# Attention on one core: five of a head's eight low probability halves on GpSimd instead of four

## The reference

```python
h = layer_norm(x, g1, b1)
q, k, v = (h @ wq1), (h @ wk1), (h @ wv1)            # 16 heads of 64
sim = einsum('bhid,bhjd->bhij', q, k) * D_HEAD ** -0.5   # 1024 x 1024 per head
attn = softmax(sim, axis=-1)
out = einsum('bhij,bhjd->bhid', attn, v)
x = x + out @ wo1 + bo1
```

## Time and profile before

| | |
|---|---|
| median of 3 runs | 2682.14 us (2680.29 to 2689.24) |
| the profiled execution | 2685.46 us, its span 2683.7 us |
| TensorE busy | 2270.3 us (85%) |
| VectorE busy | 1770.8 us (66%) |
| ScalarE busy | 1586.9 us (59%) |
| GpSimd busy | 1234.0 us (46%) |
| self-attention, four stretches | 353, 354, 357 and 352 us |
| in these 1416 us: TensorE, VectorE, ScalarE, GpSimd busy | 1308.8, 1143.4, 1113.8, 834.8 us |
| granted TensorE clock there | 0.98, 0.99, 0.98, 1.00 |

### The profile page before, as it was taken

How to read it: one execution, slowest core, us unless ns; L and a number is a source line. 1 busy time by engine, 2 the same in 40 slices (tenths; PEclk the granted TensorE clock), 3 DMA queues, 4 the chain that set the end, 5 groups by cost and what they waited for, 6 DMA issues and landing times.

```text
span 2683.7 us, 58442 instructions
## 1 busy us (share of the span) xinstructions
PE 2270.3 (85%) x24644; PEld 1437.8 (54%) x24644; DVE 1770.8 (66%) x3202; ACT 1586.9 (59%) x2124; POOL 1234.0 (46%) x756
## 2 busy tenths in 40 slices
PE   5999987779699998777869999877797999987778
PEld 2566655455365655445526665554553666554455
DVE  5888874644688887464358888746446888874643
ACT  2877774633477777363237777736334777772632
POOL 2555562640265556264026555626402655561640
PEclk8999998889799999797969999988897999997979
DMA  2212110210212121020022221102102121210200
GB/s 64 70 45 70 45 47 9 58 33 1 57 49 68 47 57 35 18 63 19 16 65 59 56 59 49 42 9 58 33 1 58 49 68 47 60 32 20 61 19 16
DMA packets 64021, 116.26 MB, mean 43 GB/s; under 512 B 16758, under 2 KB 21008, under 8 KB 63760
## 3 DMA queue, kind: packets, MB, share of 16 engines
q1 hardware_dynamic: 63760, 112.52, 16.1%
HBM read 50.77 MB, written 2.10 MB: 20 GB/s over the span
## 4 chain that ended last, share of the span: by engine, by line
PE 55%; DVE 16%; issue 7%; ACT 6%; DMA 6%; POOL 5%; SPq 4%; POOLq 2%; DVEq 0%; ACTq 0%
PE scores L687 7%; PE scores L688 6%; PE scores L689 6%; PE work L764 6%; PE scores L806 5%; PE scores L795 5%; DVE minima L1123 4%; SPq L519 3%; DVE prob L1146 3%; PE work L826 3%; PE work L830 3%; PE work L687 3%; PE work L689 3%; PE work L688 3%; PE work L828 3%
## 5 line engine op out<-in xcount | busy, mean ns | idle before, releaser
L654 POOL TENSOR_TENSOR prob<-prob 128x1024 f16<-128x1024 f32 (+1 forms) x320 | 689.3, 2155 | 753.4 <-ACT prob L990 741.1
L1123 DVE TENSOR_REDUCE minima<-work 128x1 f32<-128x512 f32 x1024 | 685.8, 685 | 112.4 <-PE work L764 97.7
L989 ACT ACTIVATE prob<-scores 128x1024 f32<-128x1024 f32 (+1 forms) x576 | 592.4, 1028 | 280.9 <-PE scores L806 258.3
L990 ACT ACTIVATE prob<-scores 128x1024 f16<-128x1024 f32 (+1 forms) x576 | 588.8, 1022 | 0.0
L826 PE MATMUL work<-vals,prob 128*128 128x65 f16 (+1 forms) x4608 | 497.1, 195 | 62.0 <-POOL prob L654 53.5
L826 PEld LDWEIGHTS work<-vals,prob 128*128 128x128 f16 (+1 forms) x4608 | 438.2, 100 | 134.6 <-POOL prob L654 67.1
L830 PE MATMUL work<-vals,prob 128*128 128x65 f16 (+1 forms) x4608 | 497.1, 197 | 0.0
L828 PE MATMUL work<-vals,prob 128*128 128x64 f16 (+1 forms) x4608 | 497.1, 195 | 0.0
L828 PEld LDWEIGHTS work<-vals,prob 128*128 128x128 f16 (+1 forms) x4608 | 436.0, 98 | 59.0 <-issue 2.9
L764 PE MATMUL work<-ka,qa 128*128 128x512 f16 x1024 | 406.2, 400 | 66.9 <-DMA kb<-staged_k 37.5
L830 PEld LDWEIGHTS work<-vals,prob 128*128 128x128 f16 (+1 forms) x4608 | 436.3, 99 | 0.0
(11 more groups left out here) (127 smaller groups left out, 4015.8 us busy)
## 6 DMA issues: line engine op xcount, KB each, us to landing
raw_odd<-in_pieces SPq DMA_DIRECT2D x40, 512.0 KB, 3.8
raw_even<-in_pairs SPq DMA_DIRECT2D x53, 384.0 KB, 3.2
qa<-staged_q SPq DMA_DIRECT2D x128, 128.0 KB, 2.3
ka<-staged_k SPq DMA_DIRECT2D x128, 128.0 KB, 2.3
qb<-staged_q SPq DMA_DIRECT2D x64, 128.0 KB, 2.3
kb<-staged_k SPq DMA_DIRECT2D x64, 128.0 KB, 2.4
qa<-qa SPq DMA_DIRECT2D x64, 128.0 KB, 2.3
raw_odd<-in_pairs SPq DMA_DIRECT2D x13, 384.0 KB, 3.2
```

Of the source, the lines that this page charges most:

```text
L654: pool.tensor_tensor(prob[1][0:kr, slot, :], prob32[0:kr, slot, :], prob[0][0:kr, slot, :], ALU.subtract).then_inc(a.polished, 1)
L989: act.activation(prob32[0:kr, n % shape.ring, :], source, ACT.Exp)
L990: act.activation(prob[0][0:kr, n % shape.ring, :], source, ACT.Exp)\
L1123: dve.tensor_reduce(minima[:, t, h:h + 1], out[:, :], AX.X, ALU.max, negate=True)\
```

## The change

The set of tiles whose low half GpSimd makes goes from (1, 3, 5, 7) to (0, 3, 4, 5, 7). VectorE makes those of tiles 1, 2 and 6 instead of 0, 2, 4 and 6. The list of steps is the same; only the engine of tiles 0, 1 and 4 changes.

```diff
 RING, LAG = 4, 3
-SELF = Shape("self", TILES, P, 2, 2, 1, (1, 3, 5, 7))
+SELF = Shape("self", TILES, P, 2, 2, 1, (0, 3, 4, 5, 7))
 CROSS = Shape("cross", 1, CTX, 1, 2, 2, ())
```

## The result

| | before | after |
|---|---|---|
| median of 15 runs each, taken side by side | 2681.20 us (2670.77 to 2694.55) | 2691.93 us (2687.75 to 2702.05) |
| the profiled execution | 2685.46 us | 2701.96 us |
| VectorE busy, GpSimd busy | 1770.8, 1234.0 us | 1713.3, 1404.2 us |
| TensorE's clock in the four self-attentions | 0.98, 0.99, 0.98, 1.00 | 0.99, 0.99, 0.98, 0.98 |

The changed kernel is slower by a ratio of 1.0045 (95% interval 1.0028 to 1.0061), that is 12 us (7.5 to 16.4). Forecast were 8.5 and a time of 2690.5. VectorE has lost 57 us of work and GpSimd has gained 170; the time follows neither sum, as expected.

What follows compares the result with a forecast made beforehand. TensorE is what the rest waits on, itself waiting for key DMA, max-reduces, shifts and GpSimd's low halves. Terms 24 - 18.5 + 8 - 3 - 2 = +8.5 us on the runs' median 2682.14 gave 2690.5 us, range 2666 to 2722.

Steps and rivals of the forecast that it cites:

- First heads: 24 first heads of pairs: tile 1's subtraction ahead of the gather delays TensorE's value product by 1.0 us each, +24 us.
- the earlier row: Row of shifts goes out 0.7 us earlier at each head's end; a few heads wait for it, -2 us.
- The two races: First heads: tile 1's subtraction finds GpSimd free, tile 2's starts before polish 3; both margins 0.1 to 0.2 us.
- Second heads: 28 heads: step 3's excess goes, -23 us; later delays at the head's end +4.5; term -18.5, between -28 and -4.
- nothing won later in VectorE comes back: First heads: step 7's first max waits for the key DMAs, so tile 4's subtraction leaving step 5 gains nothing.
- The first head of a round: 4 heads: split now behind polish 0 delays tile 1's and possibly tile 2's subtraction; +8 us, between 3 and 13.
- The last pair: 4 heads, first one bound by GpSimd: fewer subtractions get between, -1.0 at best; term -3 us, between -4 and +3.
- the race at polish 3: Rival: GpSimd goes before tile 2's subtraction in all 24 first heads, +41 us, about 2731 us; chance 0.11.
- The value product: Rival: in first heads its slack covers the gather's delay, the +24 goes, sum -15.5, 2666.5 us; chance 0.16.
- The 85 us of freed VectorE time: Rival: the 64 subtractions leaving VectorE count in full, 85 us, giving 2597 us; chance 0.03.
- The shared way as the bound: Rival: each head adds 0.91 us of exclusive VectorE/GpSimd use, +58 us, 2740 us; chance 0.04.
- The clock's rival: Rival: a second idle microsecond brings TensorE's half-speed clock in 20 more first heads, +32 on top, 2722 us; chance 0.10.

Runs made afterwards that it cites:

- the thin splits: Kernel before, with the three 1024-wide split instructions (L595 to L599) done on 32 columns only: 2621.59 us, ratio 0.9788.

## Why the prediction was right, step by step

The time and the sign were right, and so was the mechanism of the two big terms, the refine ahead of the gather in first heads and the split in front of tile 0 in second heads. Tile 4's effect in second heads had no term, and that the single terms come out as close as they do is in part luck.

- **First heads**, +24 and -2 for the earlier row: measured +22.3 with both. The gather came 1.13 later and the weight load 1.00, as worked out, in 24 of 24. The fifth exponential came only 0.81 later, 24 x 0.81 = 19.4, because the weight load is the wrong mark: before, it ran 0.21 ahead of the value product's first matmul, which waited its turn on TensorE; now it runs 0.03 ahead. From the gather's end to that matmul there were 0.46 us (2295.23 to 2295.69), of which 0.15 are the hand-over (2310.61 to 2310.76), so the slack was 0.31, and the matmul came 1.13 - 0.31 = 0.82 later in all 24. In the kernel before, and then in the changed one:

```profile
2295.69 0.19 PE L826 MATMUL work<-vals,prob 128*128 128x65 f16 x1
```

```profile
2310.76 0.19 PE L826 MATMUL work<-vals,prob 128*128 128x65 f16 x1 [0.65 <-DVE o_nat L1159]
```

  The last gap fell from 2.53 to 2.46 in the mean (-1.7). The rest, +4.6, is the step with the key DMA (3.87 to 4.06 in the mean), where 11 of the 24 heads take 0.8 to 2.6 us longer than the usual 3.23, in the kernel before as in this one; the granted clock stood at 0.50 for 14 us of that step in the 24 heads, 6 before. That these belong to the change isn't shown, so the closeness to +22 is luck. The gather was named as the cause; placing it first (above) freed the value product and gave back 0.2 of the 0.81. The refine in step 2 costs, and the gather is only the first behind it. (Of the 28 waits for the key DMA in the earlier trace rows, 24 are in such heads and 4 ahead of the rounds; the reading that all 28 such heads have one holds for the changed kernel alone, which has 32.)
- **The two races** were won in all 24 first heads, by 0.19 and 0.22 us, where 0.1 to 0.2 was reckoned.
- **Second heads**, -23: measured (4.19 - 3.37) x 28 = -23.0. The mechanism is as described; 23 was the middle of two bounds, and that it hit to the tenth is luck. What was left of the loss at the head's end was put at 0.16 each; the sum -17.1 leaves (23.0 - 17.1) / 28 = 0.21. The number hides two errors. Tile 1's refine met L596 and not L595, and L599 was over (2288.89) before tile 2's was issued: it is the first of the two that stands in the way of the next maxima. That costs +0.43 in the mean, over the three gaps behind the fourth exponential, and with the gather first, where that refine takes 1.25, it is gone (+0.05). Tile 4 then gives back 0.22 in the gap behind the seventh (3.13 to 2.91). Without tile 4 that gap is 3.14 and the second heads gain 9.7 instead of 17.1.
- **Tile 4**: "nothing won later in VectorE comes back" was said of first heads, and there it holds: TensorE's shorter wait for the shift goes into a longer one for the key DMA (above). What failed is the sentence on second heads that the shift hangs on ScalarE's merge copy. Before the change it hung on VectorE, where tile 4's refine stood in a row with what follows (1.40 us behind the step's exponential); with that refine gone it hangs on the merge copy (1.18). The prediction saw the row of shifts go out earlier and priced only the heads that wait for its DMA (-2). In second heads tile 4 is worth 6.5 us of the -17.1; with last pairs and what isn't placed it is 12 to 15, and without it the change would have cost 25.
- **The first head of a round**, +8 between 3 and 13: measured +9.9. In three of four rounds polish 3 took the way first. VectorE and GpSimd in the round at 723 us, which answers to the earlier trace rows:

```profile
730.13 2.00 DVE L1146 TENSOR_TENSOR prob<-prob 128x1024 f16<-128x1024 f32 x1
...
733.25 2.96 DVE L1146 TENSOR_TENSOR prob<-prob 128x1024 f16<-128x1024 f32 x1
```

```profile
729.40 1.64 POOL L599 TENSOR_TENSOR wp<-raw_even,wp 128x768 f16<-128x768 f32 x1
...
733.01 2.13 POOL L654 TENSOR_TENSOR prob<-prob 128x1024 f16<-128x1024 f32 x1 [1.96 <-ACT prob L990]
```

  Tile 1's refine waits for L599 (731.04) and tile 2's, issued 0.24 behind polish 3, waits until 735.1. Here a quarter of a microsecond decides over 1.7.
- **The last pair**, -3 between -4 and +3: -7.4 + 4.0 = -3.4. The wait for GpSimd's low half is 1.0 shorter in each, the "-1.0 at best" of the prediction, and by its mechanism: it is gone wherever tile 4 has left VectorE. The rest of the -7.4 and the 4.0 more in the last heads, where TensorE now waits 4.0 us for a gather behind tile 1's refine, were not in the sum and cancel by luck.

The rivals: the race at polish 3 was not lost in the 24 heads, but it was in three of the four others, by the mechanism described. The value product had 0.31 us of slack, far from the 1.13 that this rival needs. The 85 us of freed VectorE time did not count in full: tile 4 alone frees as many subtractions and gave 12. The shared way as the bound falls by the runs: a fifth polish in each head, tile 4's, makes the kernel faster. The clock's rival, 20 more stretches at 0.50, did not come: there were 11 in self-attention before and 12 after (41 and 45 us in all).

The Trainium skill's exclusive lock ("SBUF — State Buffer", Who interferes with whom) is borne out by the thin splits, which alone bring the refine from 1.71 or 3.16 back to 1.22; but what it cost was a matter of place, not of the time on it.

## What to carry to other kernels

An engine's busy time says little on what moving an instruction off it is worth: ask for each place what stands right behind the instruction, and who waits for that. Where one setting covers several kinds of iteration, work it out for each kind; here one set gave -17 us in one kind of head and +22 in the other, and choosing per kind turned +12 into -16, with tile 4 and the gather's place chosen too into -32. When a wait row is read, ask what the change takes from it as well as what it adds, and look at the wait right behind it: a wait that gets shorter is worth something only where the next one doesn't get longer by as much.

## What the runs showed of the hardware

- A VectorE subtraction that GpSimd holds up by GpSimd got the way between two GpSimd instructions: in the second head above it ran behind L596 (over at 2285.82) and ahead of L599, GpSimd's own next (held up until the subtraction ended at 2286.90). Whoever comes second pays the rest of the other's instruction, so a lead of 0.2 us decided over 0.9 us on GpSimd or 1.7 on VectorE.
- A key DMA costs SyncE 0.60 us to issue, and one more of them made a plain step 0.65 us longer (3.23 to 3.88).
